# Row sums of the adjacency matrix: some of its columns added up by ACT from a second copy in rows, and 21 more units split in the first pass

## The reference, cut to what matters

```python
h = jnp.maximum(_layernorm(x, axis=-1), 0.0)
x = x + _L0_gnn_ref(h, adj, ...)          # relu([h, adj @ h] @ W.T + b)
h = jnp.maximum(_layernorm(x, axis=-1), 0.0)
x = x + _L1_gnn_ref(h, adj, ...)          # uses rsqrt(sum(adj + eye, axis=-1))
h = jnp.maximum(_layernorm(x, axis=-1), 0.0)
x = x + _L2_gnn_ref(h, adj, ...)          # relu(adj @ states @ W.T) into a GRU cell
h = jnp.maximum(_layernorm(x, axis=-1), 0.0)
x = x + _L3_gnn_ref(h, adj, ...)          # uses 1 / sqrt(sum(A, axis=-1)), then 4 nearest rows
```

## Time and profile before

| | |
|---|---|
| median of 3 runs | 1380.79 us (1380.49 to 1380.92) |
| the profiled execution: time, span | 1382.97 us, 1381.2 us |
| PE busy | 1326.4 us (96%) |
| DVE busy | 1089.1 us (79%) |
| ACT busy | 720.8 us (52%) |
| POOL busy | 138.3 us (10%) |
| DMA | 291.46 MB, mean 211 GB/s |
| pass 0 | from the start to about 322.5 us |

### The profile page before, as it was taken

The page is one execution under the profiler, slowest core; times in us unless marked ns, Lnnn a source line. Parts: engine busy times, 40 slices in busy tenths (PEclk is TensorE's granted clock), DMA queues, the critical chain, the costliest instruction groups (busy, mean ns, idle before and its releaser), DMA issues.

```text
span 1381.2 us, 15265 instructions
## 1 busy us (share of the span) xinstructions
PE 1326.4 (96%) x5384; PEld 950.1 (69%) x5384; DVE 1089.1 (79%) x1504; ACT 720.8 (52%) x1094; POOL 138.3 (10%) x146
## 2 busy tenths in 40 slices
PE   7999999999899999999999899997999999999997
PEld 4556677778678876777877778776777777544443
DVE  7998889988999788766655898679999999623233
ACT  2332223446666577765555678556655566333232
POOL 0000000000000000000000100000000000177775
PEclk9999999999999999999999999999999999999999
DMA  9787665557876685566555889900111111699995
GB/s 347 232 261 242 232 211 198 195 184 249 313 244 228 209 326 168 189 212 218 175 196 180 306 280 340 343 1 8 54 54 46 47 45 54 224 346 362 353 359 212
DMA packets 82858, 291.46 MB, mean 211 GB/s; under 512 B 10848, under 2 KB 10976, under 8 KB 82784
## 3 DMA queue, kind: packets, MB, share of 16 engines
q1 hardware_dynamic: 78048, 280.01, 58.8%
q0 software_dynamic: 4736, 10.49, 2.4%
HBM read 286.27 MB, written 4.19 MB: 210 GB/s over the span
## 4 chain that ended last, share of the span: by engine, by line
PE 66%; DVE 29%; ACT 2%; issue 2%; DMA 1%; SPq 0%; ACTq 0%; DVEq 0%
PE ps L466 19%; PE ps L461 12%; PE ps L463 12%; PE ps L462 12%; DVE best_at L1175 9%; DVE rows_T L1171 9%; DVE A_lo L1099 5%; PE ps L536 1%; PE ps L564 1%; PE ps L565 1%; PE ps L499 1%; PE ps L505 1%; DVE hn L955 1%; PE ps L523 1%; DVE stats L940 1%
## 5 line engine op out<-in xcount | busy, mean ns | idle before, releaser
L1099 DVE TENSOR_TENSOR A_lo<-ring,A_hi 128x1024 fp32r<-128x1024 f32 x344 | 409.8, 1220 | 71.3 <-ACT A_hi L676 69.2
L676 ACT ACTIVATE A_hi<-ring 128x1024 fp32r<-128x1024 f32 x344 | 354.9, 1056 | 111.6 <-PE ps L463 90.6
L461 PE MATMUL ps<-A_hi,G_odd_hi 128*128 128x512 f32 x534 | 217.9, 408 | 2.1 <-DVE A_lo L1099 2.1
L463 PE MATMUL ps<-A_hi,G_odd_lo 128*128 128x512 f32 x534 | 209.3, 392 | 0.0
L462 PE MATMUL ps<-A_lo,G_odd_hi 128*128 128x512 f32 x534 | 208.6, 391 | 0.0
L466 PE MATMUL ps<-ring,G_last 128*128 128x512 f32 x468 | 205.7, 592 | 0.0
L676 ACT ACTIVATE scores<-ps,neg_sq 128x1024 f32<-128x1024 f32 x128 | 137.3, 1111 | 51.2 <-PE ps L637 34.0
L461 PE MATMUL ps<-A_hi,G_even_hi 128*128 128x512 f32 x386 | 162.9, 422 | 0.2 <-DVE A_lo L1099 0.2
L466 PEld LDWEIGHTS ps<-ring,G_last 128*128 128x128 f32 x468 | 88.4, 190 | 99.4 <-issue 97.5
L463 PE MATMUL ps<-A_hi,G_even_lo 128*128 128x512 f32 x386 | 150.9, 391 | 0.0
L462 PE MATMUL ps<-A_lo,G_even_hi 128*128 128x512 f32 x386 | 150.5, 390 | 0.0
(11 more groups left out here) (134 smaller groups left out, 1419.9 us busy)
## 6 DMA issues: line engine op xcount, KB each, us to landing
ring<-adj_t SPq DMA_DIRECT2D x524, 512.0 KB, 4.8
X<-x_rows SPq DMA_DIRECT2D x8, 256.0 KB, 7.4
scaled_rows<-G_last POOLq DMA_DIRECT2D x8, 256.0 KB, 2.7
landing<-scaled_rows,best_at POOLq DMA_INDIRECT x128, 5.3
out_rows<-X SPq DMA_DIRECT2D x8, 256.0 KB, 5.2
pack<-packed SPq DMA_DIRECT2D x1, 836.0 KB, 14.5
pack<-packed SPq DMA_DIRECT2D x1, 192.0 KB, 4.3
```

The lines of the kernel that those rows point to most:

```text
L461: mm(acc, G_hi[odd][:, kb, t, :], hi, start=start, stop=False)
L463: done = mm(acc, G_lo[odd][:, kb, t, :], hi, start=False, stop=stop)
L676: return nc.scalar.activation(out_ap, in_ap, func, **k)
L1099: v_.tensor_tensor(A_lo[:, s, :, :], ring[:, s, :, :], A_hi[:, slot_of(v), :, :].bitcast(fp32), ALU.subtract).then_inc(lower_ready, 1)
```

## The change

The host passes a second array, `adj_rows`: adj in plain rows, cut into pieces of 128 rows by 1024 columns (512 KB). `ROW_PIECES` names the column pieces that are added up in rows, block by block: none in blocks 0, 1 and 7, one (piece 2) in block 2, two (2 and 3) in blocks 3, 4 and 5, one (piece 3) in block 6. That is 32 pieces in all, 16.8 MB. POOL loads them through its own queue into two buffers, `row_piece`; ACT adds up each along its row with a Copy that has an accumulator (`add_piece`), into `row_sum`. DVE leaves out `add_unit` for the units that these pieces cover (96 are left of 128), and `degrees` adds `row_sum` to what PE gives. In `Plan` DVE's clock does not advance for a unit that is not added, so more units come out as split: 365 instead of 344, by block 3 more in block 2, 5 in block 3, 6 in block 4, 4 in block 5, 3 in block 6. Some handover steps of ACT, DVE and PE get a visit one later.

```diff
...
+PIECE = 1024
+ROW_PIECES = ((), (), (2,), (2, 3), (2, 3), (2, 3), (3,), ())
 LEAD = {"PE": 0, "ACT": 4, "DVE": 3}
...
+        self.sum_count, self.row_sums, n = {}, {}, 0
+        for v in self.visits[:NB * UNITS]:
+            self.sum_count[v.n], n = n, n + self.by_columns(v.b, v.u)
+        self.sum_count[NB * UNITS] = n
+        for b in range(NB):
+            parts = [(b, n, c) for n in range(TPB) for c in range(len(ROW_PIECES[b]))]
+            for i, part in enumerate(parts):
+                self.row_sums[b * UNITS + (2 * i + 1) * UNITS // (2 * len(parts))] = part
...
         return self.visits[-1]
+    def by_columns(self, b, u):
+        return u * UK * P // PIECE not in ROW_PIECES[b]
...
             if p == 0:
-                self.vector_us = max(self.vector_us, self.us - 4 * VECTOR_US) + VECTOR_US
+                self.vector_us = max(self.vector_us, self.us - 4 * VECTOR_US)
+                self.vector_us += self.by_columns(b, kb * HALVES + half) * VECTOR_US
                 split = split or b > 0 and self.vector_us + VECTOR_US <= self.us + SPLIT_US + BEHIND_US
...
         sq_aug = at("sq_aug", [P, NB, BLK], r32, sums_at)
+        row_piece = at("row_piece", [P, 2, PIECE], fp32, sums_at + 8192)
         gate_r, new, gate_z, cand = (colsum[:, i, :] for i in range(4))
...
         row_end = lambda p, b: PLAN.spans[p, b, p][1] + 1
+        pieces = [(b, n, c) for b in range(NB) for n in range(TPB) for c in range(len(ROW_PIECES[b]))]
         slot_of = lambda v: PLAN.split_count[v.n] % STAGED
...
                     sp.wait_ge(used, v.n - SLOTS + 1)
-                    if v.n - SLOTS < NB * UNITS:
-                        sp.wait_ge(summed, v.n - SLOTS + 1)
+                    before = PLAN.visits[v.n - SLOTS]
+                    if before.n < NB * UNITS and PLAN.by_columns(before.b, before.u):
+                        sp.wait_ge(summed, PLAN.sum_count[before.n] + 1)
                 sp.dma_start(ring[:, s, :, :], at_in[v.b, v.u, :, :, :]).then_inc(at_loaded[s], 16)
...
+            def add_piece(b, n, c):
+                i = pieces.index((b, n, c))
+                act.wait_ge(row_loaded[i % 2], 16 * (i // 2 + 1))
+                f(row_piece[:, i % 2, :], row_piece[:, i % 2, :], ACT.Copy,
+                  accum_out=row_sum[:, b, n, c:c + 1]).then_inc(row_summed, 1)
             def step(name, p, b):
...
                     upper(v)
+                if v.n in PLAN.row_sums:
+                    add_piece(*PLAN.row_sums[v.n])
                 for name, p, b in PLAN.due["ACT"].get(v.n, ()):
...
                 else:
-                    dve.wait_ge(summed, v.n - 1)
+                    dve.wait_ge(summed, n - 1)
                     ins = v_.tensor_tensor(half, half, ring[:, s, :, :], ALU.add)
             def fold(b):
-                dve.wait_ge(summed, UNITS * (b + 1))
+                dve.wait_ge(summed, PLAN.sum_count[UNITS * (b + 1)])
                 own.add(v_.tensor_tensor(colsum[:, 0:2, :], colsum[:, 0:2, :], colsum[:, 2:4, :], ALU.add))
...
                     dve.wait_ge(root_ready, rank[0, b])
-                v_.tensor_copy(degree[:, b, :], ps[:, AUX, 0:TPB])
-                v_.tensor_copy(deg_pair[:, 0, :], ps[:, AUX, 0:TPB])
-                v_.tensor_scalar(deg_pair[:, 1, :], ps[:, AUX, 0:TPB], 1.0, None, ALU.add).then_inc(pair_ready, 1)
+                if not ROW_PIECES[b]:
+                    own.add(v_.tensor_copy(degree[:, b, :], ps[:, AUX, 0:TPB]))
+                else:
+                    dve.wait_ge(row_summed, 1 + max(i for i in range(len(pieces)) if pieces[i][0] == b))
+                    own.add(v_.tensor_tensor(degree[:, b, :], row_sum[:, b, :, 0], ps[:, AUX, 0:TPB], ALU.add))
+                if len(ROW_PIECES[b]) == 2:
+                    own.settle()
+                    own.add(v_.tensor_tensor(degree[:, b, :], degree[:, b, :], row_sum[:, b, :, 1], ALU.add))
+                own.settle()
+                v_.tensor_copy(deg_pair[:, 0, :], degree[:, b, :])
+                v_.tensor_scalar(deg_pair[:, 1, :], degree[:, b, :], 1.0, None, ALU.add).then_inc(pair_ready, 1)
             def add_out(p, b):
...
             for v in PLAN.visits[UNITS:PLAN.rows_end]:
-                if v.feeds[0] == 0:
+                if v.feeds[0] == 0 and PLAN.by_columns(v.b, v.u):
                     add_unit(v)
...
             g.memset(eps_d2[:, :], 1e-10).then_inc(consts_set, 1)
+            for i, (b, n, c) in enumerate(pieces):
+                if i < 2:
+                    pool.wait_ge(used, b * UNITS - SLOTS)
+                else:
+                    pool.wait_ge(row_summed, i - 1)
+                pool.dma_start(row_piece[:, i % 2, :], rows_in[b, n, ROW_PIECES[b][c], :, :]).then_inc(row_loaded[i % 2], 16)
...
     at = np.ascontiguousarray(get("adj").reshape(NB, BLK, UNITS, UK, P).transpose(0, 2, 4, 3, 1))
+    rows = np.ascontiguousarray(get("adj").reshape(NB, TPB, P, N // PIECE, PIECE).transpose(0, 1, 3, 2, 4))
     w0, w1, wm = get("L0_gnn_W"), get("L1_gnn_W"), get("L2_gnn_W_msg")
...
```

More of the change, by code:

```diff
@@ L223, in settle, with gnn_stack @@
         self.eng.wait_ge(self.sem, self.n)
-def gnn_stack(nc, x_in, at_in, pack_in, scaled_rows, out):
+def gnn_stack(nc, x_in, at_in, rows_in, pack_in, scaled_rows, out):
     fp32, bf16, u32, r32 = mybir.dt.float32, mybir.dt.bfloat16, mybir.dt.uint32, mybir.dt.float32r
@@ L289, in gnn_stack @@
         degree = sb("degree", [P, NB, TPB])
+        row_sum = sb("row_sum", [P, NB, TPB, 2])
         deg_pair = sb("deg_pair", [P, 2, TPB])
@@ L322, in gnn_stack @@
         at_loaded = [sem(f"at_loaded{s}") for s in range(SLOTS)]
-        used, summed = sem("used"), sem("summed")
+        used, summed, row_summed = sem("used"), sem("summed"), sem("row_summed")
+        row_loaded = [sem(f"row_loaded{i}") for i in range(2)]
         upper_ready, lower_ready = sem("upper_ready"), sem("lower_ready")
@@ L974, in add_unit @@
             def add_unit(v):
-                s, j = v.n % SLOTS, v.n % UNITS
+                s, n = v.n % SLOTS, PLAN.sum_count[v.n]
+                j = n - PLAN.sum_count[v.b * UNITS]
                 dve.wait_ge(at_loaded[s], loaded_value(v.n))
@@ L1323 @@
     nc = bacc.Bacc("TRN2", target_bir_lowering=False, num_devices=1, dynamic_dma_scratch_size=8192)
-    arrays = {"x_rows": x, "adj_t": at, "packed": pack}
+    arrays = {"x_rows": x, "adj_t": at, "adj_rows": rows, "packed": pack}
     aps = [nc.dram_tensor(n, a.shape, fp32, kind="ExternalInput").ap() for n, a in arrays.items()]
```

## The result

The changed kernel takes 1373.61 us (median of 5 runs, 1373.16 to 1375.15) against 1380.92 us before (median of 5, the three of the table above among them); the ratio is 0.9946, with a 95% interval of 0.9935 to 0.9957. That is 7.3 us less; 6.9 were forecast.

The account below looks back on a forecast made before the run. PE alone was taken to set the pace, with DVE's work hidden behind it. Splits -7.5, block 6's wait -0.7 and block 3's stall +1.3 gave -6.9: 1380.8 to 1373.9 us, range 1371.8 to 1378.8.

Parts of the forecast that it names:

- The splits: Pass 0, blocks 2 to 6: 21 units of one pass go from 1.72 to 1.36 us, 7.5 us less on PE.
- DVE's ledger: Count of DVE's instructions between handovers: idle time before `degrees` becomes 3.2, 4.0 and 4.5 us, cover enough on average.
- One sign I named: A sign to look for in the trace: `degrees` still waiting for PE in every block.
- The handovers: Blocks 4 to 6: no loss taken; margin 0.35 us in blocks 5 and 6, over 1 in block 4.
- its wait for `hTs`: Block 6: a shared visit before `operand` removes PE's wait of 0.69 us for `hTs`, -0.7 us.
- its stall: Block 3: three `A_hi` and two pieces between `roots` and `hTs` make PE wait at `operand`, +1.3 us.
- The pieces: ACT 1.1 us each, POOL issue 0.75; nearest landings 4.8 and 5.3, costly past 8; hidden but for block 3.
- DMA as the bound: Rival: in blocks 3 to 5 DMA engines become the bound, slower below about 300 GB/s; 1384 at 290 to 300 upward; chance 0.10.
- My 325 to 329 for a full share: Blocks 3 to 5: full DMA rate in GB/s, worked out from shares of 0.71, 0.67 and 0.63.
- POOL against DVE: Rival: POOL's issues and DVE hold each other up through a port, costing 6.3 us; 1380.2, no change; chance 0.07.
- The handovers eating the gain: Rival: thin margins and late pieces cost 1 us in each of blocks 3 to 6, about 1377; chance 0.13.
- nothing but a shift: A sign to look for: from 320 us on, behind pass 0, the trace is only shifted.

Follow-up runs that it names:

- sums_behind_htS: The changed kernel with five sums of block 3 at other visits, so no piece stands between roots and hTs after visit 53; 1377.2 us, ratio 0.9964.
- dma_doubled: The changed kernel plus a second 512 KB transfer to HBM scratch behind each piece, awaited by ACT; on another chip, ratio 1.0018 to the kernel before.
- whole_units_gone: one_sum_behind with the plan's allowance for DVE (BEHIND_US) at 1.22 instead of 0, 369 units split; 1377.06 us, ratio 0.9970.
- one_sum_behind: The changed kernel with one sum of block 3 moved from visit 57 to 58, behind hTs; 1374.92 us, ratio 0.9952.
- changed_again: The changed kernel unedited, timed a second time on another chip; 1374.93 us, ratio 0.9956.

## Why the prediction was right, step by step

**The splits.** 21 x 0.36 = 7.5 us. Shown by the run without the splits, 0.9999, and by blocks 4 and 5, where nothing else changed on PE: 2.11 for six splits and 1.42 for four, 0.35 each. With the 0.9 of block 6 and the 1.1 of block 3 below, the terms as measured give -7.3; the 6.9 forecast was short by 0.2 in each of the two.

**DVE's ledger.** The direction was right, and the half without pieces shows that the ledger is needed: PE waits where it says. It was too small by 0.6, 1.5 and 1.3 us there, so the idle time of DVE that it gives, 3 to 4.5 us, is good to 0.6 to 1.5 us and no closer. One sign I named was wrong: `degrees` no longer waits for PE in every block. It does in the stretches of blocks 3 and 7 (4.48 and 3.98), and in those of blocks 4 to 6 it has no idle time, since the room now lies ahead of the `lower` before it, where DVE waits for `A_hi`. That `lower` ended just in time in blocks 5 and 6 and 0.5 us late in block 4, where the margin was over 1.

**The handovers.** PE waited in none of blocks 4 to 6 for `hn`. The last `hn` ended 1.2, 1.2 and 0.7 us before `h_transposes` started (163.25, 199.83 and 239.62 against 164.45, 201.02 and 240.28), where over 1, 0.35 and 0.35 were forecast; in block 5 a copy of colsum, with the next instruction 0.57 us behind it, stands where an add of 1.14 was counted. Block 6 lost its wait for `hTs`, 0.7 forecast: its length fell by 2.01, of which three splits are 1.07, so 0.9. The forecast took the recorded wait of 0.69 for this term, though it had worked out 1.0 that the block lost. Block 3 got its stall, +1.3 forecast; PE's recorded wait is 0.85, and the block's length says 5 x 0.357 - 0.66 = 1.1. The sum gave 1.4, rounded down to 1.3, and so was too large by 0.3: an `A_hi` next to another instruction of ACT took 0.95 and not 1.0, three times, and a piece 1.04 and not 1.1, twice. In blocks 3 and 6 alike the length moved by some 0.25 more than PE's recorded wait. Moving one sum by one visit took the stall away.

**The pieces.** 1.04 against 1.1 us on ACT; POOL's issue 0.53 against 0.75; landing 6.8 us against 4.8 and 5.3, near the 8 at which I said it would cost. ACT waited up to 3.2 us for a piece, where I had said no more than 1. In the changed kernel it is hidden, and with five sums moved, four of them closer together, it cost 3.5 us in the traced execution. That wait is a bound I hadn't worked out: with two buffers and 6.8 us to land, plus the issue and the sum, two pieces need some 8 us.

**The rivals.** DMA as the bound: the mean rate of blocks 3 to 5 was 338 GB/s, forecast at 340, and the shares were 0.90 to 0.95. My 325 to 329 for a full share, worked out from share and rate at part load, was too low: block 4 moved 354 GB/s at 0.95, and the doubled load 415 to 422, of which a part was of another kind. POOL against DVE: not seen, `lower` and the total being the same with the pieces on SP's queue. The handovers eating the gain: not in this kernel, but PE's waits at the handovers are what cost in sums_behind_htS, dma_doubled and whole_units_gone.

**What lies behind pass 0.** I had said nothing but a shift. The trace is 2.7 us shorter there, which was no part of the sum; the medians differ by 7.3, close to the 7.1 of pass 0.

## What to carry to other kernels

Where one engine is full and the planner gives it cheaper work at another's cost, the gain is the number of pieces of work by the difference of their durations in the trace, once the other engines' ledgers between two synchronising steps show room; test the two halves apart, for each alone may be worth nothing or less. A planner that counts one engine's time will put its savings on the next one: count every engine's instructions between the two handover steps that PE waits for, and not its share of the span. An instruction that waits for a transfer holds up what stands behind it in the same program: keep such instructions away from the steps of a chain. A transfer's landing time, with its issue and its use added, divided by the number of its buffers sets how close its users may stand, here some 4 us.

## What was unexpected of the hardware

DMA share and rate are not proportional. In the earlier trace rows a share of 0.71 went with 233 GB/s, which looked like 328 at full; with two queues loaded the same engines moved 354 GB/s at 0.95 and 415 to 422 at 1.02 in the same blocks. The second load is not the first made larger (two queues, and in the doubled one transfers from HBM to HBM), and these runs don't separate what of this makes the difference. But a full rate worked out from a share at part load was too low here: the 354 GB/s that were moved at 0.95 are already more than the 328.

PE's granted clock is a part of the scatter of the total. Behind some of the places where PE waited a stretch runs at the lower clock, and which places are hit differs between executions of the same work. Between 550 and 572 us, in pass 2, PE waits 1.1 us for `hn` and 0.7 for `hTs` in both profiled executions; the kernel before then ran at a granted clock of 0.66 from 570 to 575 us, and the changed one, 8 us earlier, at 1.00. Before, then after:

```profile
560.00:570.00 10.00, 8.18 (x40) 6.37 (x39) 9.33 (x23) 6.67 (x8) 0.00 (x0) 1.00 0.83 264
570.00:575.00 5.00, 5.00 (x21) 3.55 (x20) 2.83 (x6) 3.64 (x8) 0.00 (x0) 0.66 0.27 106
```

```profile
560.00:570.00 10.00, 9.09 (x39) 5.65 (x39) 5.36 (x9) 7.24 (x12) 0.00 (x0) 1.00 0.35 121
570.00:580.00 10.00, 10.00 (x44) 8.08 (x43) 9.24 (x11) 8.30 (x9) 0.00 (x0) 1.00 0.74 241
```

With the two levels of 1.2 and 2.4 GHz, 0.66 is 2/3 of the stretch at the lower and 1/3 at the higher, and PE does 1.7 us less in it. That is most of the 2.7 us by which the two profiled spans differ behind pass 0; the rest stays open. one_sum_behind, which behind pass 0 is the same program as the changed kernel and has the same two waits, shows 0.66 from 560 to 565 us, where the changed kernel shows 1.00. The clock isn't the whole of the scatter, though: changed_again took 1372.83 us at a mean of 0.996 and 1376.92 at 0.993, but one_sum_behind 1374.18 at 0.993 and 1375.34 at 0.996. It also stays open why block 0, which no edit touches, took from 37.35 to 38.90 us in the profiled executions.
